# Cross attention: one VectorE instruction takes the score maxima of two heads over two PSUM banks

## The chip, the cores and the metric

The kernel runs on one core of one Trainium2 chip. The metric is the device time of one execution in microseconds (us). The core's engines are TensorE (PE; its weight loads are listed as PEld), VectorE (DVE), ScalarE (ACT), GpSimd (POOL) and SyncE (SP), which issues most DMAs. Each engine works through its own list of instructions in order and waits on semaphores that other engines raise.

## The reference

A decoder layer of 8 batches of 256 tokens and 128 features: self attention with a relative position bias, a cross attention block over 1601 context tokens with 16 heads of size 8, which is followed by a second self attention and a feed-forward part, and at last a mixture of eight experts. The change lies mainly in the first attention of the block:

```python
def _mha(x, ctx, mask, qw, qb, kw, kb, vw, vb):
    q = _split_heads(x @ qw + qb)          # 8 x 256 x 16 heads x 8
    k = _split_heads(ctx @ kw + kb)        # 8 x 1601 x 16 x 8
    v = _split_heads(ctx @ vw + vb)
    scores = jnp.einsum('bqhd,bkhd->bhqk', q, k) / np.sqrt(D // H)
    if mask is not None:
        scores = scores + mask
    probs = jax.nn.softmax(scores, axis=-1)
    out = jnp.einsum('bhqk,bkhd->bqhd', probs, v)
    return out.reshape(x.shape[0], x.shape[1], D)
```

## The kernel before

The kernel runs phase after phase: self attention "A" (with bias), cross attention (`phase_cross`), self attention "S", a tail and the experts. Queries and keys are held as three bf16 parts each, whose products are added by the rows of one matmul; two heads stand in partitions 0 to 53 and 64 to 117 (`half` 0 and 1), so that matmuls of the two halves can run side by side.

Cross attention works through 64 units g (8 batches, `b`, of 8 pairs of heads, `p`). A unit computes its scores twice:

- as **grains**, with the queries on the partitions: 16 products of 128 queries with about 401 keys (2 heads `s`, 2 query tiles `qt`, 4 chunks of the 1601 keys). Each fills one of four PSUM banks (`GRAIN`). VectorE takes the maximum of each (`maxima`, L1436) into `MG`, then `negate` (L1443) joins the chunks' maxima into the negated row maximum, GpSimd's `split_maxima` makes three bf16 parts `MP` of it, TensorE turns these (`max_rows`, "m") and ScalarE copies them into three rows of the queries (`place_maxima`). The maximum is so subtracted by the score product itself.
- as **score tiles**, with the keys on the partitions: 13 tiles of 128 keys (the last has 65). One bank of the ring `RING` (banks 4, 5 and `PX`) takes two products of 256 queries (L1238); ScalarE takes the exponential (`exponentials`, L1356) into `PT`, one of 8 buffers.

The **V products** (L1258) follow in three bursts per unit: tiles 0 to 3, 4 to 7 and 8 to 12, here burst 0, 1 and 2. They add into `k.PO`; ScalarE then copies the sums (`read_sums`, L1372).

The order of all engines' work is one list, `cross_plan(p)`, gone through once per step; each engine takes from it the entries that are its own. An entry ("g", i, 2) in step n belongs to unit n + 2, ("s", t, 0) to unit n, ("m", 0, 1) to unit n + 1. At place j (0 to 12) the list has the score tile j + 3 of the unit (from j = 10 on, tiles 0 to 2 of the next), then a round of preparing the next batch at j = 5 and 10, then, at j = 3, 7 and 12, a burst, with "m" ahead of burst 1, and then one or two grains. So two grains stand right behind burst 0 and two behind burst 1. The rounds by step of a batch: turning the context in steps 0 and 1, keys in 2 and 3, values in 4 and 5, none in 6 and 7. Step 0 also has "c" at j = 1: TensorE's batch sums (L228), VectorE's reciprocal and product (L1449, L1451). The ring's banks go in turn to scores, "m", "c" and rounds, so each of these waits until what had the bank three turns before has been read.

`grain(g, u)` waits until the maximum of the grain four before has been taken. `grain_order` writes out which head and chunk each grain has, so that halves alternate on TensorE.

In self attention "A" a unit has four grains with VectorE's maxima in `MG` (L988); VectorE negates them into `MN` (`negate`, L1001) and GpSimd splits them (L1028 to L1045). "S" negates in the reduction itself (L994).

Of the kernel before, what the change touches and what calls it, by code (L numbers as in the profile page):

```python
# [115 lines left out]
def allocate(k):  # L116
# [20 lines left out]
    k.BANK = [k.stack.enter_context(nc.psum_tensor(f"bank{i}", [128, 512], F32)) for i in range(8)]  # L137
    k.RING = [bank[:, :] for bank in k.BANK]
# [612 lines left out]
def phase_self(k, name):  # L751
# [12 lines left out]
    dve_plan = [("g", 0, 3), ("g", 1, 3), ("g", 2, 3), ("m", 0, 2), ("g", 3, 3), ("neg", 0, 3), ("c", 0, 0)]  # L764
# [20 lines left out]
    with ExitStack() as st:  # L785
# [181 lines left out]
        def _(v):  # L967
# [47 lines left out]
            if bias:  # L1015
                actions["neg"] = negate
            else:
                actions["m"] = lambda u, i: copy_maxima(nc.vector.tensor_copy, v, u, (1,), m_rows_second)
# [3 lines left out]
        def _(pl):  # L1022
# [7 lines left out]
            def split_maxima(u, i):  # L1030
                if bias:
                    pl.wait_ge(neg_ready, u + 1)
                else:
# [25 lines left out]
def cross_plan(p):  # L1059
# [3 lines left out]
    T, G, LEAD = NTILES, 16, 3  # L1063
# [4 lines left out]
    for j in range(T):  # L1068
# [6 lines left out]
        if j == 1 and p == 0:  # L1075
            plan.append(("c", 0, 0))
        if j in bursts:
            if bursts[j] == 1:
                plan.append(("m", 0, 1))
            plan.append(("v", bursts[j], 0))  # L1080
        plan += [("g", g, 2) for g in range(G * (j + 1) // T if j else 0, min(G, G * (j + 2) // T))]
    return plan + [("o", 0, 0), ("neg", 0, 2), ("split", 0, 2)]


def grain_order(chunks):

    rest = [[(s, qt, u, a, w) for qt in range(QT) for u, (a, w) in enumerate(chunks)] for s in range(2)]
# [34 lines left out]
def phase_cross(k):  # L1122

    nc = k.nc
    T, N, G = NTILES, NCTX, 16
# [9 lines left out]
    NG = len(GRAIN)  # L1135
# [9 lines left out]
    with ExitStack() as st:  # L1145
# [6 lines left out]
        MG = k.sb("MG", [128, 4, 4, 4], stack=st)  # L1152
# [32 lines left out]
        def _(pe):  # L1185
# [20 lines left out]
            def grain(g, u):  # L1206
                n = G * g + u
                b, p = batch_of(g)
                s, qt, _, a, w = grains[u]
                half = slice(HALF * s, HALF * s + CROSS_ROWS)  # L1210
                if n >= NG:
                    pe.wait_ge(m_read, n - NG + 1)
# [3 lines left out]
                if p == 0 and u == 0 and b % 2 == 0:  # L1216
                    pe.wait_ge(qk_in[b // 2], Q_LOADS)
                if u == 0:
# [208 lines left out]
        def _(v):  # L1427
            nc.vector.memset(k.PO[:, :], 0.0).then_inc(psum_cleared, 1)

            def maxima(g, u):  # L1430
                n = G * g + u
                s, qt, chunk, a, w = grains[u]
                if u == 0 and g >= 4:
                    v.wait_ge(neg_ready, g - 3)
                v.wait_ge(m_ready, n + 1)
                nc.vector.tensor_reduce(MG[:, g % 4, 2 * s + qt, chunk:chunk + 1], GRAIN[n % NG][:, 0:w],  # L1436
                                        AX.X, ALU.max).then_inc(m_read, 1)

            def negate(g, i):
# [3 lines left out]
                nc.vector.tensor_reduce(MN[:, g % 4, :], MG[:, g % 4, :, :], AX.X, ALU.max,  # L1443
# [912 lines left out]
```

## Time and profile before

| | before |
|---|---|
| median of 3 runs | 1321.23 us (1316.71 to 1325.92) |
| span of the profiled execution | 1324.9 us |
| mean TensorE clock granted | 0.924 of full speed |
| PE busy | 1104.3 us (83%) |
| DVE busy | 1018.2 us (77%) |
| ACT busy | 869.6 us (66%) |
| POOL busy | 403.8 us (30%) |

The time of the profiled execution itself is not listed apart from its span; the span lies inside the range of the three runs. Busy time of an engine counts each moment once, though instructions overlap at their ends; a single instruction's duration runs from its start to its end. Start times are counted from the start of the span. The words in brackets at the end of a timeline row are the engine's idle time ahead of it and what ended it.

### The profile page before, as it was taken

Reading aid. Unit: us, or ns where it says so; the run is one execution under the profiler, and the core shown is the slowest. Engines: PE = TensorE matmul, PEld = TensorE weight load, DVE = VectorE, ACT = ScalarE, POOL = GpSimd, SP = SyncE. Lnnn points to the kernel's source line nnn. Section 1 sums busy time; section 2 is a strip of 40 time slices with the busy share of each in tenths; the row PEclk is TensorE's granted clock in tenths of the full one; section 3 lists DMA queues with packets and bytes.
Section 4 is the critical chain, followed back from the end, with each engine's and each line's share of the span. In section 5 each row is a group of like instructions: output and inputs, shape, how many; then the busy total and the mean of one; then the engine's idle time right before and its main releaser. Section 6 shows DMA issues by size and latency. Waiting matters only on the chain. (4 is left out here: it accounts for less than half of the span.)

```text
span 1324.9 us, 33276 instructions
## 1 busy us (share of the span) xinstructions
PE 1104.3 (83%) x12028; PEld 602.7 (45%) x12028; DVE 1018.2 (77%) x2779; ACT 869.6 (66%) x1764; POOL 403.8 (30%) x832
## 2 busy tenths in 40 slices
PE   5799995699999999999999999986688878178894
PEld 2344443244444444444444444433344436167773
DVE  7488857588889898898988889956699968755554
ACT  3488873187887878788788787882488744233443
POOL 3211113223050320405023040021624227545552
PEclk9699997699999999999999999997799989588997
DMA  6970005513232132311323113002740022111113
GB/s 164 213 144 30 2 2 138 133 56 84 67 82 68 39 93 84 72 57 34 101 78 81 49 30 85 21 2 58 149 87 2 2 96 72 56 29 39 39 37 111
DMA packets 76648, 92.31 MB, mean 70 GB/s; under 512 B 8463, under 2 KB 62711, under 8 KB 76488
## 3 DMA queue, kind: packets, MB, share of 16 engines
q1 hardware_dynamic: 72392, 83.90, 25.1%
q0 software_dynamic: 2496, 5.12, 1.5%
q8 instruction: 98, 1.61, 0.5%
q10 hardware_dynamic: 1600, 1.18, 0.3%
q14 instruction: 62, 0.51, 0.1%
HBM read 64.37 MB, written 27.02 MB: 69 GB/s over the span
## 5 line engine op out<-in xcount | busy, mean ns | idle before, releaser
L1436 DVE TENSOR_REDUCE MG<-bank 128x1 f32<-128x401 f32 (+1 forms) x1024 | 515.4, 566 | 75.3 <-PE bank L1220 73.6
L1356 ACT ACTIVATE PT<-bank 128x512 f32<-128x512 f32 (+1 forms) x624 | 334.6, 597 | 64.3 <-PE bank L1238 63.8
L1238 PE MATMUL bank<-QP,KP 54*128 54x256 bf16 (+1 forms) x1664 | 252.4, 274 | 16.3 <-DVE CAT L1451 4.1
L1220 PE MATMUL bank<-KP,QP 54*128 54x401 bf16 (+1 forms) x1024 | 237.0, 344 | 14.8 <-DMA KP<-ctx_k_parts 9.6
L1258 PE MATMUL bank<-PT,VP 128*9 128x256 f32 (+1 forms) x2688 | 197.3, 367 | 0.8 <-ACT XT L1356 0.8
L1511 POOL TENSOR_TENSOR MP<-MN,ZERO 128x4 bf16<-128x4 f32 x128 | 26.4, 206 | 440.8 <-DVE MN L1443 435.8
L1238 PEld LDWEIGHTS bank<-QP,KP 54*128 54x128 bf16 (+1 forms) x1664 | 110.4, 96 | 108.3 <-ACT PT L1356 24.4
L1220 PEld LDWEIGHTS bank<-KP,QP 54*128 54x128 bf16 x1024 | 75.5, 94 | 125.0 <-DVE MG L1436 94.4
L1356 ACT ACTIVATE XT<-bank 128x512 f32<-128x512 f32 (+1 forms) x208 | 116.2, 599 | 20.3 <-PE bank L1238 19.9
L896 PE MATMUL bank<-QP,KP 51*128 51x256 bf16 x512 | 95.7, 281 | 33.6 <-ACT QP L827 8.8
L1258 PEld LDWEIGHTS bank<-PT,VP 128*9 128x9 f32 (+1 forms) x2688 | 76.0, 90 | 57.6 <-issue 20.4
L863 PE MATMUL bank<-KP,QP 51*128 51x256 bf16 x512 | 97.8, 287 | 4.3 <-DVE MN L994 1.4
L988 DVE CUSTOM_DVE_ANT_0 JUNK<-bank,UQ 128x256 bf16<-128x256 f32 x256 | 92.1, 420 | 6.8 <-PE bank L863 6.6
L951 ACT ACTIVATE XT<-bank 128x512 f32<-128x512 f32 x128 | 74.1, 604 | 32.6 <-PE bank L896 32.0
L1258 PE MATMUL bank<-XT,VP 128*9 128x256 f32 (+1 forms) x896 | 91.2, 367 | 0.0
L994 DVE TENSOR_REDUCE MN<-bank 128x2 f32<-128x512 f32 x128 | 81.8, 685 | 4.2 <-POOL MP L1045 1.2
L1028 POOL TENSOR_TENSOR MP<-MN,ZERO 128x8 bf16<-128x8 f32 x128 | 26.4, 206 | 187.8 <-DVE MN L1001 112.4
L896 PEld LDWEIGHTS bank<-QP,KP 51*128 51x128 bf16 x512 | 33.2, 95 | 103.4 <-issue 43.4
L2041 PE MATMUL bank<-WUP,XP 128*128 x234 | 67.8, 427 | 14.6 <-DVE XP L2210 13.5
L827 ACT COPY QP<-bank 3x512 bf16<-3x512 bf16 x96 | 54.8, 571 | 32.4 <-PE bank L932 32.0
L1364 ACT COPY QP<-bank 3x256 bf16<-3x256 bf16 x128 | 45.3, 354 | 26.5 <-DMA q_parts<-PT 25.7
L2218 DVE TENSOR_TENSOR AC<-SI,bank 128x512 f32<-128x512 f32 x39 | 26.8, 688 | 45.5 <-issue 20.7
(281 smaller groups left out, 2007.5 us busy)
## 6 DMA issues: line engine op xcount, KB each, us to landing
KP<-ctx_k_parts SPq DMA_DIRECT2D x128, 100.1 KB
ctx_k_parts<-KPARTS SPq DMA_DIRECT2D x16, 600.4 KB
KP<-ctx_k_parts SPq DMA_DIRECT2D x128, 59.4 KB
CN<-in_ctx SPq DMA_DIRECT2D x8, 768.0 KB
RAW<-in_w_gate_up SPq DMA_DIRECT2D x8, 512.0 KB, 3.8
QP<-q_parts SPq DMA_DIRECT2D x20, 192.0 KB
ctx_k_parts<-KPARTS SPq DMA_DIRECT2D x16, 200.1 KB
UQ<-bias_table SPq DMA_DIRECT2D x4, 768.0 KB, 8.5
```

The source lines that it names most:

```text
L827: last = copy(k.QP[rows, p:p + 2, b * S:(b + 1) * S], PM[:, :].bitcast(BF16)[rows, 0:2 * S].rearrange("r (j n) -> r j n", j=2))
L863: last = nc.tensor.matmul(bank[:, S * qt:S * (qt + 1)], k.QP[rows, p, a:a + 128], k.KP[rows, p, b * S:(b + 1) * S], start=True, stop=True)
L896: last = nc.tensor.matmul(bank[:, S * t:S * (t + 1)], k.KP[half(s), p, a:a + 128], k.QP[half(s), p, b * S:(b + 1) * S], start=not bias, st ...
L951: nc.scalar.activation(PT[n % 8], SCORE[n % 3][:, :], ACT.Exp).then_inc(exp_done, 1)
L988: last = nc.vector.tensor_tensor_reduce(out=JUNK[:, 2 * (n % 2) + q, :], in0=bank[:, S * q:S * (q + 1)], in1=k.UQ[:, 2 * p + s, 128 * q:12 ...
L994: nc.vector.tensor_reduce(MN[:, u % 3, j, s, :], bank[:, :].rearrange("p (q n) -> p q n", q=QT), AX.X, ALU.max, negate=True).then_inc(grai ...
L1220: nc.tensor.matmul(GRAIN[n % NG][:, 0:w], k.QP[half, p, b * S + 128 * qt:b * S + 128 * (qt + 1)], k.KP[half, p, a:a + w], start=True, stop ...
L1238: return nc.tensor.matmul(bank[0:rows[t], S * at:S * (at + 1)], k.KP[half, p, 128 * t:128 * t + rows[t]], k.QP[half, p, b * S:(b + 1) * S] ...
L1258: last = nc.tensor.matmul(k.PO[32 * c:32 * c + HD + 1, q:q + w], VP[b % 2][0:rows[t], t, 2 * p + s, :], PT[(T * g + n) % NP][0:rows[t], S ...
L1356: nc.scalar.activation(PT[n % NP][0:rows[t], :], bank_of("s", g, t)[0:rows[t], :], ACT.Exp).then_inc(exp_done, 1)
L1436: nc.vector.tensor_reduce(MG[:, g % 4, 2 * s + qt, chunk:chunk + 1], GRAIN[n % NG][:, 0:w], AX.X, ALU.max).then_inc(m_read, 1)
L2041: last = nc.tensor.matmul(bank[j % 2], XP[:, j % 2, a, :], WUP[:, bass.ds(e, 1), b, n0:n0 + FF].rearrange("p a n -> p (a n)"), start=(n == ...
```

## The change

1. Banks 0 to 3 are allocated as one tensor `k.FOUR`, so that an instruction can read two neighbouring banks. `DOUBLE` are its two halves.
2. In cross attention a grain is now a double: the products of both heads for one query tile and one chunk, one in each bank of `DOUBLE[n % 2]`. A unit has 8 instead of 16. TensorE waits once, until the double two before has been read, and signals once, with the second product. VectorE takes both maxima with one reduction of 128x2x401. `MG` is laid out anew for it.
3. `cross_plan` names the places of the doubles: after the scores of j = 0, 1, 3, 4, 6, 7, 9 and 11 and ahead of what else stands there, so that doubles 2 and 5 stand ahead of bursts 0 and 1, and nothing of the kind stands behind a burst. "neg" and "split", which closed a step with unit n + 2, now come after the first double of the next step.
4. In self attention "A" the negation is done by GpSimd, at the head of `split_maxima`, instead of VectorE.

```diff
-    k.BANK = [k.stack.enter_context(nc.psum_tensor(f"bank{i}", [128, 512], F32)) for i in range(8)]
+    k.FOUR = k.stack.enter_context(nc.psum_tensor("bank", [128, 4, 512], F32))
+    more = [k.stack.enter_context(nc.psum_tensor(f"bank{i}", [128, 512], F32)) for i in range(4, 8)]
+    k.BANK = [k.FOUR[:, i, :] for i in range(4)] + [bank[:, :] for bank in more]
...
-    dve_plan = [("g", 0, 3), ("g", 1, 3), ("g", 2, 3), ("m", 0, 2), ("g", 3, 3), ("neg", 0, 3), ("c", 0, 0)]
+    dve_plan = [("g", 0, 3), ("g", 1, 3), ("g", 2, 3), ("m", 0, 2), ("g", 3, 3), ("c", 0, 0)]
...
-            def negate(u, i):
-                v.wait_ge(grain_read, 4 * u + 4)
-                if u >= 3:
-                    v.wait_ge(max_split, 4 * (u - 2))
-                nc.vector.tensor_scalar(MN[:, u % 3, :, :, :], MG[:, u % 3, :, :, :], -1.0, None,
-                                        ALU.mult).then_inc(neg_ready, 1)
...
             def split_maxima(u, i):
-                if bias:
-                    pl.wait_ge(neg_ready, u + 1)
-                else:
-                    pl.wait_ge(grain_read, 4 * u + 4)
+                pl.wait_ge(grain_read, 4 * u + 4)
                 if u >= 3:
                     pl.wait_ge(m_turned, u - 2)
+                if bias:
+                    flat = MG[:, u % 3, :, :, :].rearrange("p j s q -> p (j s q)")
+                    nc.gpsimd.tensor_tensor(MN[:, u % 3, :, :, :].rearrange("p j s q -> p (j s q)"),
+                                            ZERO[:, :].broadcast_to(list(flat.shape)), flat,
+                                            ALU.subtract).then_inc(neg_ready, 1)
+                    pl.wait_ge(neg_ready, u + 1)
...
-    T, G, LEAD = NTILES, 16, 3
+    T, LEAD = NTILES, 3
+    doubles = {0: 0, 1: 1, 3: 2, 4: 3, 6: 4, 7: 5, 9: 6, 11: 7}
...
+        if j in doubles:
+            plan.append(("g", doubles[j], 2))
+        if j == 0:
+            plan += [("neg", 0, 1), ("split", 0, 1)]
         if j in bursts:
             if bursts[j] == 1:
                 plan.append(("m", 0, 1))
             plan.append(("v", bursts[j], 0))
-        plan += [("g", g, 2) for g in range(G * (j + 1) // T if j else 0, min(G, G * (j + 2) // T))]
-    return plan + [("o", 0, 0), ("neg", 0, 2), ("split", 0, 2)]
+    return plan + [("o", 0, 0)]
...
     order, half = [], 0
-    for what, i, _ in cross_plan(PAIRS - 1):
+    for what, d, _ in cross_plan(PAIRS - 1):
         if what == "s":
-            half = 1 - i % 2 if i < NTILES - 1 else 0
+            half = 1 - d % 2 if d < NTILES - 1 else 0
         if what == "g":
-            order.append((rest[half] or rest[1 - half]).pop(0))
-            half = 1 - half
+            order.append((half, *places[d]))
...
-                if n >= NG:
-                    pe.wait_ge(m_read, n - NG + 1)
+                if n >= 2:
+                    pe.wait_ge(m_read, n - 1)
...
-                nc.tensor.matmul(GRAIN[n % NG][:, 0:w], k.QP[half, p, b * S + 128 * qt:b * S + 128 * (qt + 1)],
-                                 k.KP[half, p, a:a + w], start=True, stop=True).then_inc(m_ready, 1)
+                for s in (first, 1 - first):
+                    half = slice(HALF * s, HALF * s + CROSS_ROWS)
+                    last = nc.tensor.matmul(DOUBLE[n % 2][:, s, 0:w],
+                                            k.QP[half, p, b * S + 128 * qt:b * S + 128 * (qt + 1)],
+                                            k.KP[half, p, a:a + w], start=True, stop=True)
+                last.then_inc(m_ready, 1)
...
-                nc.vector.tensor_reduce(MG[:, g % 4, 2 * s + qt, chunk:chunk + 1], GRAIN[n % NG][:, 0:w],
+                nc.vector.tensor_reduce(MG[:, g % 4, :, qt, chunk], DOUBLE[n % 2][:, :, 0:w],
                                         AX.X, ALU.max).then_inc(m_read, 1)
```

## Rows read from the trace of the kernel before

**Rows 1.** Windows: busy us of each engine, granted clock, DMA share, GB/s.
```profile
265.00:925.00 660.00, 607.38 (x7121) 293.05 (x7119) 562.38 (x1238) 518.93 (x1087) 159.56 (x373) 0.98 0.23 62
```

**Rows 2.** Waits from 300 to 900 us: who for whom, total, times, longest.
```profile
PEld bank L1220 <- DVE MG L1436: 79.5, 192, 0.6
...
DVE MG L1436 <- PE bank L1220: 57.7, 135, 1.5
```

**Rows 3.** Timeline of PE in a plain step: start, us, instructions.
```profile
407.53 0.62 PE L1258 MATMUL bank<-XT,VP 128*9 128x256 f32 x8
...
408.52 0.34 PE L1220 MATMUL bank<-KP,QP 54*128 54x401 bf16 x2
...
408.70 0.27 PE L1238 MATMUL bank<-QP,KP 54*128 54x256 bf16 x1
...
409.77 0.39 PE L1238 MATMUL bank<-QP,KP 54*128 54x256 bf16 x2
...
410.36 0.40 PE L1258 MATMUL bank<-PT,VP 128*9 128x256 f32 x2
...
412.91 0.82 PE L1220 MATMUL bank<-KP,QP 54*128 54x401 bf16 x2
...
413.72 0.62 PE L1258 MATMUL bank<-XT,VP 128*9 128x256 f32 x8
...
414.92 0.28 PE L1238 MATMUL bank<-QP,KP 54*128 54x256 bf16 x1
```

**Rows 4.** Timeline of ACT in the same step.
```profile
409.11 0.60 ACT L1356 ACTIVATE PT<-bank 128x512 f32<-128x512 f32 x1 [0.48 <-PE bank L1238]
...
412.02 2.52 ACT L1356 ACTIVATE PT<-bank 128x512 f32<-128x512 f32 x5 [0.26 <-PE bank L1238]
415.06 0.37 ACT L1372 COPY OT<-bank 128x256 f32<-128x256 f32 x1 [0.52 <-PE bank L1258]
```

**Rows 5.** Timeline of DVE in the same step.
```profile
406.47 0.17 DVE L1443 TENSOR_REDUCE MN<-MG 128x4 f32<-128x16 f32 x1
...
408.90 2.50 DVE L1436 TENSOR_REDUCE MG<-bank 128x1 f32<-128x401 f32 x5 [0.21 <-PE bank L1220]
411.80 3.46 DVE L1436 TENSOR_REDUCE MG<-bank 128x1 f32<-128x401 f32 x7 [0.40 <-PE bank L1220]
```

**Rows 6.** The page's groups of instructions: busy us, mean ns, idle before.
```profile
L1436 DVE TENSOR_REDUCE MG<-bank 128x1 f32<-128x401 f32 (+1 forms) x1024 | 515.4, 566 | 75.3 <-PE bank L1220 73.6
...
L994 DVE TENSOR_REDUCE MN<-bank 128x2 f32<-128x512 f32 x128 | 81.8, 685 | 4.2 <-POOL MP L1045 1.2
```

**Rows 7.** Timeline of ACT: the copies of the sums, one a step.
```profile
343.82 0.37 ACT L1372 COPY OT<-bank 128x256 f32<-128x256 f32 x1 [0.51 <-PE bank L1258]
...
356.00 0.37 ACT L1372 COPY OT<-bank 128x256 f32<-128x256 f32 x1 [0.40 <-PE bank L1258]
...
365.49 0.37 ACT L1372 COPY OT<-bank 128x256 f32<-128x256 f32 x1 [0.63 <-PE bank L1258]
...
385.47 0.37 ACT L1372 COPY OT<-bank 128x256 f32<-128x256 f32 x1 [0.49 <-PE bank L1258]
...
396.19 0.37 ACT L1372 COPY OT<-bank 128x256 f32<-128x256 f32 x1 [0.49 <-PE bank L1258]
...
406.27 0.37 ACT L1372 COPY OT<-bank 128x256 f32<-128x256 f32 x1 [0.58 <-PE bank L1258]
```

**Rows 8.** Timeline of PE in a batch's first step and in a values step.
```profile
348.53 0.39 PE L1238 MATMUL bank<-QP,KP 54*128 54x256 bf16 x2 [0.58 <-DVE CAT L1451]
...
390.61 0.23 PE L1269 MATMUL bank<-IDB,MP 128*3 128x128 bf16 x2 [0.57 <-DVE VP L1461]
```

**Rows 9.** Timeline of DVE in a batch's first step.
```profile
348.38 2.01 DVE L1436 TENSOR_REDUCE MG<-bank 128x1 f32<-128x401 f32 x4
```

**Rows 10.** Timeline of POOL: last operation of a split.
```profile
407.57 0.21 POOL L1524 TENSOR_TENSOR MP<-MN,MP 128x4 bf16<-128x4 f32 x1
```

**Rows 11.** Timeline of DVE in self attention "A", behind the negation.
```profile
147.39 0.06 DVE L986 MEMSET TOUCH<- 1x1 f32 x1 [0.90 <-PE bank L863]
```

More of the change, by code:

```diff
@@ L136, in allocate @@
     k.HALF = k.sb("HALF", [128, NT])
-    k.BANK = [k.stack.enter_context(nc.psum_tensor(f"bank{i}", [128, 512], F32)) for i in range(8)]
-    k.RING = [bank[:, :] for bank in k.BANK]
+    k.FOUR = k.stack.enter_context(nc.psum_tensor("bank", [128, 4, 512], F32))
+    more = [k.stack.enter_context(nc.psum_tensor(f"bank{i}", [128, 512], F32)) for i in range(4, 8)]
+    k.BANK = [k.FOUR[:, i, :] for i in range(4)] + [bank[:, :] for bank in more]
+    k.RING = list(k.BANK)
     k.PO, k.PX = k.BANK[6], k.BANK[7]
@@ L1014, in _ @@
             actions = {"g": maxima, "c": divide}
-            if bias:
-                actions["neg"] = negate
-            else:
+            if not bias:
                 actions["m"] = lambda u, i: copy_maxima(nc.vector.tensor_copy, v, u, (1,), m_rows_second)
@@ L1080, in cross_plan @@
             plan.append(("v", bursts[j], 0))
-        plan += [("g", g, 2) for g in range(G * (j + 1) // T if j else 0, min(G, G * (j + 2) // T))]
-    return plan + [("o", 0, 0), ("neg", 0, 2), ("split", 0, 2)]
+    return plan + [("o", 0, 0)]
 def grain_order(chunks):
-    rest = [[(s, qt, u, a, w) for qt in range(QT) for u, (a, w) in enumerate(chunks)] for s in range(2)]
+    places = [(qt, u, a, w) for qt in range(QT) for u, (a, w) in enumerate(chunks)]
     order, half = [], 0
-    for what, i, _ in cross_plan(PAIRS - 1):
+    for what, d, _ in cross_plan(PAIRS - 1):
         if what == "s":
-            half = 1 - i % 2 if i < NTILES - 1 else 0
+            half = 1 - d % 2 if d < NTILES - 1 else 0
         if what == "g":
-            order.append((rest[half] or rest[1 - half]).pop(0))
-            half = 1 - half
+            order.append((half, *places[d]))
     return order
@@ L1124, in phase_cross @@
     nc = k.nc
-    T, N, G = NTILES, NCTX, 16
+    T, N, G = NTILES, NCTX, 8
     rows = [min(128, N - 128 * t) for t in range(T)]
@@ L1204, in take_bank, with grain @@
                 return RING[n % 3]
-            def grain(g, u):
-                n = G * g + u
+            def grain(g, d):
+                n = G * g + d
                 b, p = batch_of(g)
-                s, qt, _, a, w = grains[u]
-                half = slice(HALF * s, HALF * s + CROSS_ROWS)
-                if n >= NG:
-                    pe.wait_ge(m_read, n - NG + 1)
+                first, qt, _, a, w = grains[d]
+                if n >= 2:
+                    pe.wait_ge(m_read, n - 1)
                 if n == 0:
@@ L1215, in grain @@
                     pe.wait_ge(q_taken, 4)
-                if p == 0 and u == 0 and b % 2 == 0:
+                if p == 0 and d == 0 and b % 2 == 0:
                     pe.wait_ge(qk_in[b // 2], Q_LOADS)
-                if u == 0:
+                if d == 0:
                     pe.wait_ge(kp_in[p], LOADS * (b + 1))
-                nc.tensor.matmul(GRAIN[n % NG][:, 0:w], k.QP[half, p, b * S + 128 * qt:b * S + 128 * (qt + 1)],
-                                 k.KP[half, p, a:a + w], start=True, stop=True).then_inc(m_ready, 1)
+                for s in (first, 1 - first):
[4 more added lines that the diff above has]
+                last.then_inc(m_ready, 1)
             def scores(g, i):
@@ L1428, in _, with maxima @@
             nc.vector.memset(k.PO[:, :], 0.0).then_inc(psum_cleared, 1)
[L1430 to L1433, printed above, removed]
+            def maxima(g, d):
+                n = G * g + d
+                _, qt, chunk, a, w = grains[d]
+                if d == 0 and g >= 4:
                     v.wait_ge(neg_ready, g - 3)
                 v.wait_ge(m_ready, n + 1)
-                nc.vector.tensor_reduce(MG[:, g % 4, 2 * s + qt, chunk:chunk + 1], GRAIN[n % NG][:, 0:w],
+                nc.vector.tensor_reduce(MG[:, g % 4, :, qt, chunk], DOUBLE[n % 2][:, :, 0:w],
                                         AX.X, ALU.max).then_inc(m_read, 1)
@@ L1514, in split_maxima @@
                 pl.wait_ge(neg_ready, g + 1)
+                x, parts = MN[:, g % 4, :], [MP[:, g % 4, :, a] for a in range(3)]
                 if g >= 4:
                     pl.wait_ge(m_turned, g - 3)
-                x, parts = MN[:, g % 4, :], [MP[:, g % 4, :, a] for a in range(3)]
                 copy(parts[0], x).then_inc(max_split, 1)
```

10 lines of the change are left out of this document (4 added, 6 removed).

## The prediction

> **What bounds the kernel now.** I read the trace from coarse to fine: the windows, the waits, then one step of each kind in the timelines. Only cross attention matters for most of the change, and it is the stretch from 265 to 925 us. VectorE is busy there for 562 of 660 us, TensorE for 607, ScalarE for 519 [rows 1]. None is full, so the order of waits decides. The waits go round in a circle: TensorE's weight loads for grains wait 79.5 us for maxima, and the maxima wait 57.7 us for grains [rows 2]. A saving on either engine is worth something only where its wait ends last.
>
> So I took one plain step (no round of the next batch) and measured from the start of burst 2, at 404.93, which is 8.79 before the row at 413.72 [rows 3]. Below, times after a + sign count from the last start of burst 2, and Vn is burst n. V0 starts at 407.53, +2.60. It stands behind the score of tile 6, which waits for the exponential of tile 3, which waits for the copy of the sums at V2 +1.34 (415.06 against 413.72) [rows 3, 4]. V1 starts at 410.36, +5.43, through score 7, its exponential at 409.11 and the next exponential, for which the bank of the transposed maxima waits [rows 3, 4]. V2 starts at 413.72, +8.79. It is held by grain 15 (the second of the two at 412.91, which start 0.48 apart), which is started only when the maximum of grain 11 is out; the chain of exponentials alone (412.02, the next 0.48 later) would have let tile 2's score, and with it V2, start 0.26 sooner [rows 3 to 5]. VectorE has gaps of its own in this step: before a run of five reads and before a run of seven it waits 0.21 and 0.40 us beyond the tail of a read [rows 5]. Both lie behind bursts. The loop is thus mostly TensorE to ScalarE and back; VectorE closes it only before V2.
>
> **The reads.** Seven reads take 3.46 us, five 2.50 [rows 5]: (3.46 - 2.50)/2 = 0.48 us from start to start, against 0.566 from start to end [rows 6]. A read of 512 columns takes 0.685 [rows 6], so a column costs (685 - 566)/111 = 1.07 ns. A double adds 401 columns: 0.99 us to its end, 0.91 to the next start. Eight save 8 x (0.966 - 0.91) = 0.45 us of VectorE a step. No row has a read over two banks. One bound is the time of two reads, 0.48 + 0.566 = 1.05, or 1.13 if both pay in full; the other is 0.89, if 0.03 of the 0.119 us between the two forms is the price of L994's second output and a column costs 0.80 ns. I take 0.99, as L994 is nearest: it too reads two runs and writes two maxima.
>
> The Trainium skill, "Perfetto Trace Analysis", Optimizing Scalar/DVE Operations, gives VectorE about 125 ns of overhead per instruction on PSUM and advises grouping where the engine is saturated; it also says that where an engine is not saturated but makes others wait, smaller instructions let work finish sooner, which speaks against this change. Starts 0.48 us apart for 401 columns leave 0.05 to 0.07 us of overhead that blocks the next read, half of what the page gives; by the page 8 x 0.125 = 1.0 us of VectorE a step would be saved, an estimate from that page.
>
> **What is later: V0.** In the new order D0 follows score 3, D1 score 4, and D2 stands after score 6, ahead of V0. D2 uses D0's banks and waits for D0's read. TensorE returns from V2 at +1.20 (414.92 against 413.72) [rows 3]. D0's second half waits for two score products of 0.11 each, starts at +1.42, takes 0.34 and is seen 0.04 later: VectorE reads D0 from +1.80 to +2.79. D2 starts 0.06 later (TensorE's delay after such a wait: an exponential ends at 409.11 + 0.60, the score that waits for it starts at 409.77 [rows 3, 4]) and V0 0.26 behind it (its 0.17 of streaming and 0.09 of change-over). V0: +3.11 instead of +2.60, 0.50 later. In exchange the pair of grains between V0 and score 7 is gone, which costs 408.70 - 408.52 = 0.18 [rows 3]: score 7 is 0.32 later.
>
> **V1.** In a plain step score 7's exponential and the next would allow V1 0.32 later. But D5, which now stands before the maxima's transposes and V1, waits for the read of D3. D3 starts after V0: ready at V0 + 0.98 + 0.22 + 0.38 = +4.69, read by +5.68, D5 at +5.74, V1 0.28 later: +6.02, so 0.57 to 0.59 later. The pair behind V1 (0.18) is gone too: scores 11 and 12 are 0.39 later.
>
> **V2.** The 0.26 of slack in the exponentials takes part of the 0.39, since D7 waits for D5's read, long out. Plain step: +0.14. That is 19 steps (two in each of seven batches, five in the last, not counting two steps that make no maxima).
>
> **Steps with rounds** have these periods, between copies of the sums [rows 7]: 12.18, 9.49, twice 9.99, 10.72, 10.08. In them V1 waits for the round's own chain (its bank must be taken before the maxima's transposes: idle 0.57 behind VP [rows 8]), which starts 0.18 sooner behind V0 as the pair is gone, so V1 is 0.50 - 0.18 = 0.32 later and score 11 is 0.14 later. Where the last part is set by the exponentials (the second and sixth step) the step is +0.14. Where it is set by TensorE after the second round (third to fifth), three single grains become one double: 0.34 is won there, -0.20 each. In the first step VectorE's reciprocal and product hold the bank of score 7 until 348.53, 0.15 after the next read starts [rows 8, 9]. D3 now stands between scores 7 and 8 and waits for D1's whole read, 0.99 from 348.38: score 8 starts 0.41 later, V1 0.57, score 11 0.39; 0.13 of slack remains, +0.26. The last batch has this step without rounds: +0.6, since nothing hides D5's wait.
>
> **Sum.** A batch: 0.26 + 0.14 - 0.20 x 3 + 0.14 + 0.14 x 2 = +0.22; seven give +1.6, the last 0.6 + 5 x 0.14 = +1.3. Cross attention: +2.9 us.
>
> **Edits that cost nothing.** "neg" and its split follow D0 now, one read later. The split ends 1.31 us after the negation starts (407.57 + 0.21 against 406.47 [rows 5, 10]), so at about +4.0, and its reader stands ahead of V1 near +6. The order of halves stays alternating, and the two halves of a double run side by side as two grains did (two in 0.34 us [rows 3]). In the first attention VectorE's negation goes, 32 of 0.17 us, and GpSimd does one more operation of 0.2 us for a unit. VectorE waits 0.90 us for grains right after that negation [rows 11], so the 0.17 ends as longer idle time; the split is late by 0.08 to 0.1 and is read 1.5 us after it is done. Without that cover 32 x 0.1 = 3 us either way. The key loads follow scores, and the POOL and SP queues keep their order.
>
> The profiled span is 1324.9 us; the runs have 1316.7 to 1325.9 and no time stands with that execution itself. A difference carries over: 1321.2 + 2.9 = 1324.
>
> **Rivals.** (a) Faster: VectorE is the bound, as the 79.5 us of weight loads behind maxima suggest [rows 2]. Then a step gains 0.45 us, x 62 = 28: 1293. Against it stand VectorE's own 57.7 us of waits and its gaps behind V0 and V1. By the skill's overhead, 1.0 us a step, it would be about 60 us, an estimate from "Perfetto Trace Analysis"; the row at 3.46 us for seven reads disagrees.
> (b) Faster: D2 and D5 find their banks free, because D0 is read sooner than I walk, and only the two pairs behind the bursts are gone. 2 x 0.18 x 62 = 22 us: 1299. Against it: D0 cannot start before V2 is through, and its read alone takes about one microsecond.
> (c) Slower: a read over two banks costs as much as two, 1.13 us. The place is D0's read before V0, once in each of 62 steps, and D3's (or D1's) read again in the 27 plain and first steps: 89 x 0.14 = 12 us on top of 2.9: 1336. It decides from about 1.1 us a read. For it: nothing in the trace shows such a read. Against it: L994 reads in two runs with no extra price per run.
> (d) The change does not do what it says if the doubles are read as two instructions; that is the price of (c) at 1.05, 1329, and lies in the range.
>
> **Chances.** Forecast with (d) 0.61, its own range 1314 to 1332; (a) 0.08; (b) 0.11; (c) 0.20. A measurement of this kernel tells about 1% from no change, its three runs being 0.7% apart, so the forecast counts as same, (a) and (b) as faster and (c) as slower. The range 1298 to 1338 takes in (b), the forecast and (c), and leaves (a) out.
>
> **What would show it.** In the profile after: 512 reads at L1436's place of 0.99 us; V0 3.1 us behind the start of V2 in steps without batch sums; V1 6.0 behind V2 in plain steps and 0.3 later than before in steps with rounds; periods of 8.9 in plain steps and 9.8 in the steps that make keys; VectorE with less busy time (by about 30 us) and more waiting for TensorE; L1001's negation gone with the first attention as long as before. The forecast is wrong if V0 stays at 2.6, or if the read is not near 0.99.

## The result, and the profile after

After the change the kernel takes 1334.0 us (median of 4 runs, 1331.2 to 1336.9), before it 1320.9 (4 runs beside them, 1316.7 to 1325.9): a ratio of 1.010, 95% interval 1.0066 to 1.0132, so about 13 us slower. The forecast was 2.9 us slower. The profiled executions span 1329.4 and 1324.9 us, only 4.5 apart, because the one of after came to cross attention 3.7 us earlier (first V product at 262.4 instead of 266.1) and was 3.7 us shorter behind it. Neither is put down to the change: over all twelve traces, whose kernels hardly differ outside cross attention, the first V product comes between 261.9 and 266.1, and what stands behind the last burst takes 423.7 to 429.9 us. Between the first start of burst 0 and the last start of burst 2 it took 640.7 us instead of 628.9. These 11.8 us are to be explained.

The page of after, its parts 1 and 5. VectorE is busy 977.4 us, 40.8 less than before, and the reads over two banks take 988 ns:

```profile
PE 1089.8 (82%) x12028; PEld 592.9 (45%) x12028; DVE 977.4 (74%) x2235; ACT 870.2 (65%) x1764; POOL 412.8 (31%) x864
...
L1438 DVE TENSOR_REDUCE MG<-bank 128x2 f32<-128x802 f32 (+1 forms) x512 | 489.6, 988 | 120.3 <-PE bank L1220 117.6
```

The windows (busy us of each engine, granted clock, DMA share, GB/s) over cross attention, where VectorE was busy 85% of the time [rows 1] and is now busy 79%:

```profile
265.00:903.00 638.00, 582.74 (x6976) 275.77 (x6975) 504.94 (x660) 510.39 (x1069) 154.13 (x364) 0.99 0.22 61
```

The waits from 300 to 900 us:

```profile
DVE MG L1438 <- PE bank L1220: 99.7, 153, 2.0
...
PEld bank L1220 <- DVE MG L1438: 45.3, 85, 0.8
...
PE bank L1220 <- DVE MG L1438: 20.8, 79, 0.6
```

TensorE waits less for maxima, 45.3 + 20.8 us where the weight loads alone had 79.5, while VectorE waits 99.7 us for scores instead of 57.7 [rows 2]. VectorE has become cheaper and waits more, yet the whole is longer. The totals can't say why, as they don't tell which of the waits a burst stands behind. That is seen only in a step.

TensorE in a plain step. Burst 2 starts at 410.25, D0 at 411.46 and 411.68, D2 at 413.17, V0 at 413.45, D5 at 416.07, V1 at 416.36, V2 at 419.30:

```profile
410.25 0.62 PE L1260 MATMUL bank<-XT,VP 128*9 128x256 f32 x8
...
411.45 0.28 PE L1240 MATMUL bank<-QP,KP 54*128 54x256 bf16 x1
...
411.68 0.33 PE L1220 MATMUL bank<-KP,QP 54*128 54x401 bf16 x1
...
413.17 0.34 PE L1220 MATMUL bank<-KP,QP 54*128 54x401 bf16 x2 [0.25 <-DVE MG L1438]
413.45 0.81 PE L1260 MATMUL bank<-PT,VP 128*9 128x256 f32 x9
...
416.07 0.34 PE L1220 MATMUL bank<-KP,QP 54*128 54x401 bf16 x2 [0.17 <-DVE MG L1438]
...
416.36 0.40 PE L1260 MATMUL bank<-PT,VP 128*9 128x256 f32 x2
...
419.30 0.62 PE L1260 MATMUL bank<-PT,VP 128*9 128x256 f32 x8
```

VectorE in the same step:

```profile
412.12 0.99 DVE L1438 TENSOR_REDUCE MG<-bank 128x2 f32<-128x802 f32 x1 [0.87 <-PE bank L1220]
413.03 0.16 DVE L1445 TENSOR_REDUCE MN<-MG 128x4 f32<-128x16 f32 x1
413.11 4.71 DVE L1438 TENSOR_REDUCE MG<-bank 128x2 f32<-128x802 f32 x5
418.40 1.89 DVE L1438 TENSOR_REDUCE MG<-bank 128x2 f32<-128x802 f32 x2 [0.59 <-PE bank L1220]
```

VectorE stands idle for 0.87 us until D0 is computed, reads it until 413.11, and 0.06 us after that D2 starts, with V0 0.28 behind it. (The group of 4.71 us from 413.11 is five reads, of which the first is D1's.) The "[0.25 <-DVE MG L1438]" in the row of D2 and the "[0.17 ...]" in that of D5 are the two new places at which all of TensorE stands still for VectorE. Relative to V2:

| plain step | before | forecast | after |
|---|---|---|---|
| D0's read starts | - | +1.80 | +1.87 |
| V0 | +2.60 | +3.11 | +3.20 |
| V1 | +5.43 | +6.02 | +6.11 |
| V2 (the period) | +8.78 | +8.92 | +9.05 |

The copies of the sums by ScalarE, one a step, to set against those of before [rows 7]:

```profile
339.36 0.37 ACT L1374 COPY OT<-bank 128x256 f32<-128x256 f32 x1 [0.26 <-PE bank L1260]
...
351.80 0.37 ACT L1374 COPY OT<-bank 128x256 f32<-128x256 f32 x1 [0.26 <-PE bank L1260]
...
361.54 0.37 ACT L1374 COPY OT<-bank 128x256 f32<-128x256 f32 x1 [0.63 <-PE bank L1260]
...
371.45 0.37 ACT L1374 COPY OT<-bank 128x256 f32<-128x256 f32 x1 [0.16 <-PE bank L1260]
...
392.00 0.37 ACT L1374 COPY OT<-bank 128x256 f32<-128x256 f32 x1 [0.32 <-PE bank L1260]
...
402.34 0.37 ACT L1374 COPY OT<-bank 128x256 f32<-128x256 f32 x1 [0.63 <-PE bank L1260]
...
411.59 0.37 ACT L1374 COPY OT<-bank 128x256 f32<-128x256 f32 x1 [0.27 <-PE bank L1260]
```

The copies don't all wait alike, so I take the periods below from the starts of burst 2 in the trace's timeline of TensorE. They repeat from batch to batch to 0.02 us wherever the clock is full and no transfer is awaited:

| step of a batch | 0 | 1 | 2 | 3 | 4 | 5 | 6 | 7 | batch |
|---|---|---|---|---|---|---|---|---|---|
| before | 12.17 | 9.49 | 9.99 | 9.99 | 10.72 | 10.08 | 8.78 | 8.78 | 80.0 |
| after | 12.44 | 9.75 | 9.91 | 9.91 | 10.64 | 10.34 | 9.05 | 9.05 | 81.1 |
| difference | +0.27 | +0.26 | -0.08 | -0.08 | -0.08 | +0.26 | +0.27 | +0.27 | +1.1 |
| forecast | +0.26 | +0.14 | -0.20 | -0.20 | -0.20 | +0.14 | +0.14 | +0.14 | +0.2 |

The batches from the second to the last took 1.27, 1.07, 2.37, 2.83, 1.06, 0.99 and 3.03 us longer than the same ones of before. 1.07 is the table's step pattern. Most of what lies above it is in first steps of 13.75 to 13.77 us instead of 12.44, in the fourth, fifth and seventh batch (the seventh has such a step before the change too, 13.58 for 12.17, so the difference there is only 0.99), and in that of the last; two seventh steps add 0.2 and 0.4. The windows of two first steps after, each from V0 to just ahead of V2, at full clock and at reduced clock, and the last part of the latter, from V1 on; the column behind the busy times is the granted clock:

```profile
423.60:431.70 8.10, 6.62 (x74) 3.12 (x72) 7.22 (x9) 6.24 (x13) 0.00 (x0) 1.00 0.15 48
504.70:514.10 9.40, 7.95 (x74) 3.52 (x72) 7.17 (x9) 6.26 (x13) 0.00 (x0) 0.82 0.23 70
509.54:514.14 4.60, 4.51 (x40) 2.07 (x39) 2.41 (x4) 3.09 (x9) 0.00 (x0) 0.66 0.28 86
```

These two windows hold the same 74 matmuls and the same 9 and 13 operations of VectorE and ScalarE, and the second is 1.3 us longer. TensorE is busy 1.33 us more in it, the other two no more than in the first. TensorE ran part of it at the lower of its two levels, 1.2 GHz instead of 2.4. Before the change the same happened once in seven first steps (the windows of before):

```profile
426.60:434.70 8.10, 7.10 (x80) 3.35 (x81) 7.53 (x14) 6.53 (x14) 0.00 (x0) 1.00 0.16 49
746.70:756.10 9.40, 8.46 (x76) 3.74 (x74) 7.61 (x14) 6.69 (x14) 0.00 (x0) 0.82 0.13 45
```

After it, four times in seven, the last one in the eighth batch (13.07 us, granted clock 0.87). What a first step has ahead of that part is in the timelines of VectorE and TensorE, here of the one at full clock; the one with the fall has the same two stops of TensorE, 0.69 and 0.51 us:

```profile
423.06 1.76 DVE L1451 RECIPROCAL REC<-bank 128x256 f32<-128x256 f32 x1 [0.82 <-PE bank L230]
```

```profile
425.34 0.39 PE L1240 MATMUL bank<-QP,KP 54*128 54x256 bf16 x2 [0.70 <-DVE CAT L1453]
...
426.24 0.34 PE L1220 MATMUL bank<-KP,QP 54*128 54x398 bf16 x2 [0.51 <-DVE MG L1438]
```

The reciprocal runs ahead of D1's read, and with it VectorE's product (0.42 us), which frees the bank of score 7. TensorE stands still for 0.70 us for the bank of score 7, and right after it for another 0.51 us, which is new, for D1's read. Before, the first wait is there with 0.58 us [rows 8].

### The profile page after: what moved, and what is told of

It is laid out like the page before. It is cut to its first block and busy times, and to the rows that moved or that the text cites. A ratio compares the mean times of both kernels' runs of the same rounds, so it can differ in the third digit from the quotient of the medians.

```text
span 1329.4 us, 32735 instructions
## 1 busy us (share of the span) xinstructions
PE 1089.8 (82%) x12028; PEld 592.9 (45%) x12028; DVE 977.4 (74%) x2235; ACT 870.2 (65%) x1764; POOL 412.8 (31%) x864
## 5 line engine op out<-in xcount | busy, mean ns | idle before, releaser
L1438 DVE TENSOR_REDUCE MG<-bank 128x2 f32<-128x802 f32 (+1 forms) x512 | 489.6, 988 | 120.3 <-PE bank L1220 117.6
L1240 PE MATMUL bank<-QP,KP 54*128 54x256 bf16 (+1 forms) x1664 | 265.7, 276 | 25.8 <-DVE CAT L1453 4.9
L1220 PE MATMUL bank<-KP,QP 54*128 54x401 bf16 (+1 forms) x1024 | 221.2, 344 | 36.5 <-DVE MG L1438 26.5
L1240 PEld LDWEIGHTS bank<-QP,KP 54*128 54x128 bf16 (+1 forms) x1664 | 99.7, 95 | 188.9 <-ACT PT L1358 90.4
L1513 POOL TENSOR_TENSOR MP<-MN,ZERO 128x4 bf16<-128x4 f32 x128 | 26.4, 206 | 461.0 <-DVE MN L1445 456.0
L2102 ACT ACTIVATE SI<-bank 128x512 f32<-128x512 f32 x39 | 23.3, 598 | 54.5 <-PE bank L2043 45.2
```

Source lines behind the costliest of these rows:

```text
L1220: last = nc.tensor.matmul(DOUBLE[n % 2][:, s, 0:w], k.QP[half, p, b * S + 128 * qt:b * S + 128 * (qt + 1)], k.KP[half, p, a:a + w], start= ...
L1240: return nc.tensor.matmul(bank[0:rows[t], S * at:S * (at + 1)], k.KP[half, p, 128 * t:128 * t + rows[t]], k.QP[half, p, b * S:(b + 1) * S] ...
L1438: nc.vector.tensor_reduce(MG[:, g % 4, :, qt, chunk], DOUBLE[n % 2][:, :, 0:w], AX.X, ALU.max).then_inc(m_read, 1)
```

## The experiments

The theory that I took into them, from here on W: **the cost is the wait of D2 for the read of D0, which holds V0, and that of D5 for the read of D3, which holds V1**. Rivals: O, the order is the whole cost and the width of the read nothing; R, the width of the read matters, since each waiting product waits for both banks; N, the negation on GpSimd costs something.

### 1. The negation alone

The kernel before, with the change's fourth part only: in self attention "A" GpSimd negates.

```diff
-dve_plan = [("g", 0, 3), ("g", 1, 3), ("g", 2, 3), ("m", 0, 2), ("g", 3, 3), ("neg", 0, 3), ("c", 0, 0)]
+dve_plan = [("g", 0, 3), ("g", 1, 3), ("g", 2, 3), ("m", 0, 2), ("g", 3, 3), ("c", 0, 0)]
...
+                    nc.gpsimd.tensor_tensor(MN[:, u % 3, :, :, :].rearrange("p j s q -> p (j s q)"),
+                                            ZERO[:, :].broadcast_to(list(flat.shape)), flat,
+                                            ALU.subtract).then_inc(neg_ready, 1)
```

> The kernel before with part 4 of the change alone: GpSimd negates the maxima of self attention A. Theory W (the doubles ahead of bursts 0 and 1 wait for reads of VectorE and hold the bursts): this part costs nothing, 1321 within 3 us, self attention A as long as before. Rival A (the negation on GpSimd costs part of the 13 us): 1325 or more.

Measured: 1321.2 us (10 runs), ratio 0.999 (0.997 to 1.0011), and every step of cross attention as before. The window of self attention "A" in this kernel, and then in the one before:

```profile
40.00:187.00 147.00, 133.35 (x1916) 63.63 (x1916) 106.81 (x647) 113.80 (x211) 32.88 (x160) 0.92 0.36 79
```

```profile
40.00:187.00 147.00, 133.33 (x1912) 63.88 (x1916) 112.70 (x685) 113.72 (x210) 26.98 (x130) 0.92 0.37 79
```

VectorE has 5.9 us less to do in it, GpSimd 5.9 more, and TensorE, which is 91% busy, does the same work in the same time. The negation costs nothing, so N falls, and the whole cost lies in cross attention.

### 2. Each double read by two reductions

```diff
-                nc.vector.tensor_reduce(MG[:, g % 4, :, qt, chunk], DOUBLE[n % 2][:, :, 0:w],
-                                        AX.X, ALU.max).then_inc(m_read, 1)
+                for s in (0, 1):
+                    last = nc.vector.tensor_reduce(MG[:, g % 4, s:s + 1, qt, chunk], DOUBLE[n % 2][:, s, 0:w],
+                                                   AX.X, ALU.max)
+                last.then_inc(m_read, 1)
```

> The changed kernel, but each double is read by two instructions of one bank each, and only the second signals. Theory W: the pair takes 0.48 + 0.57 = 1.05 us instead of 0.99, so burst 0 starts 0.06 later (3.26 us behind the start of burst 2) and in plain steps burst 1 another 0.06: plain step 9.17, in all 1334 + 6 = 1340. Rival L (an instruction over two banks is itself what costs): faster than the changed kernel, near 1325.

Measured: 1335.0 us, 1.0116 (1.0073 to 1.0159). A plain step takes 9.17 us, V0 at +3.26. The new wait in the timeline of TensorE:

```profile
491.24 0.34 PE L1220 MATMUL bank<-KP,QP 54*128 54x401 bf16 x2 [0.31 <-DVE MG L1439]
```

D2 waits 0.31 us instead of 0.25, as the two reads end 0.06 us later than the one. A batch at full clock takes 81.8 us, 0.75 more than after the change. The steps came as expected. The total, expected at 1340, came out 5 us lower: in the profiled execution this kernel had two falls of the clock in first steps against four, and the interval is some 6 us to either side. As a price of the wide read, 0.988 us against 1.05, it is worth 0.06 us in each of the two waits, and only because those waits are there.

### 3. The order alone

The kernel before, with its single reads and four single banks, and the grains at the places of the change.

```diff
+    doubles = {0: 0, 1: 1, 3: 2, 4: 3, 6: 4, 7: 5, 9: 6, 11: 7}
...
+        if j in doubles:
+            plan += [("g", 2 * doubles[j], 2), ("g", 2 * doubles[j] + 1, 2)]
+        if j == 0:
+            plan += [("neg", 0, 1), ("split", 0, 1)]
...
-        plan += [("g", g, 2) for g in range(G * (j + 1) // T if j else 0, min(G, G * (j + 2) // T))]
-    return plan + [("o", 0, 0), ("neg", 0, 2), ("split", 0, 2)]
+    return plan + [("o", 0, 0)]
```

> The kernel before with single grains, four banks and one read a grain, but the places of the change: two grains where a double stands, ahead of the bursts, and the negation after the first two. Theory W: the second grain ahead of burst 0 waits only for the second read, which ends 0.17 sooner than a double's: burst 0 at 3.03 behind burst 2 instead of 3.20, burst 1 at 2.82 behind it instead of 2.92, plain step 8.8, in all about 1324. Rival O (the order alone is the whole cost, the double nothing): 1334, plain step 9.05.

Measured: 1334.8 us, 1.0111 (1.007 to 1.0151). A plain step takes 9.03 us, V0 at +3.12. TensorE around the wait, V2 being at 484.21, and VectorE's reads for it:

```profile
487.05 0.34 PE L1224 MATMUL bank<-KP,QP 54*128 54x401 bf16 x1
...
487.32 0.62 PE L1262 MATMUL bank<-XT,VP 128*9 128x256 f32 x8
...
490.30 0.40 PE L1262 MATMUL bank<-PT,VP 128*9 128x256 f32 x2
```

```profile
485.94 1.06 DVE L1440 TENSOR_REDUCE MG<-bank 128x1 f32<-128x401 f32 x2 [1.02 <-PE bank L1224]
```

Two single reads, begun with the first half of D0, end at 487.00, +2.79. The second grain of the pair ahead of V0 starts 0.05 later. I had expected 8.8 us from W, with this pair costing less than the double, and O's 9.0 came. So **the order is the whole cost**: with half-wide reads and four banks to itself the order costs as much as the change (a batch at full clock takes 80.9 us against 81.1). R falls. The wait that W names is still there; it is only nearly as long for the second of two single reads (V0 at +3.12) as for one wide one (+3.20).

### 4. Both waiting doubles behind their bursts

```diff
-    doubles = {0: 0, 1: 1, 3: 2, 4: 3, 6: 4, 7: 5, 9: 6, 11: 7}
+    doubles = {0: 0, 1: 1, 4: 3, 6: 4, 9: 6, 11: 7}
+    behind = {3: 2, 7: 5}
...
+        if j in behind:
+            plan.append(("g", behind[j], 2))
```

> The changed kernel with doubles 2 and 5 directly behind bursts 0 and 1 instead of ahead of them. Theory W: burst 0 is back at 2.60 behind burst 2, burst 1 at about 2.97 behind it (score 10 now waits behind double 4), burst 2 at 3.11: plain step 8.68, in all 1316 to 1320. Rival L (the read over two banks is the cost): still above 1330.

Measured: 1323.4 us, 0.9995 (0.9967 to 1.0024), as fast as before. A plain step takes 8.63 us, V0 at +2.60 and V1 at +5.53: both waits are gone, the step is 0.42 shorter than after the change and 0.15 shorter than before. The total is above the 1316 to 1320 expected. A first step took 12.46 us at full clock, but five of seven had a fall of the clock and took 13.03 to 13.78. In first steps V0 to V1 is still 4.75 us (before 4.32), as D3 waits for D1's read behind the reciprocal. The sixth step of a batch also takes 10.40 instead of 10.08, so that even at full clock a batch is 79.9 us, hardly less than the 80.0 of before.

### 5 and 6. One of the two behind its burst

Number 5 has D2 behind V0 and D5 ahead of V1, number 6 the reverse.

```diff
+    doubles = {0: 0, 1: 1, 4: 3, 6: 4, 7: 5, 9: 6, 11: 7}
+    behind = {3: 2}
```

```diff
+    doubles = {0: 0, 1: 1, 3: 2, 4: 3, 6: 4, 9: 6, 11: 7}
+    behind = {7: 5}
```

> The changed kernel with double 2 alone moved behind burst 0; double 5 stays ahead of burst 1. Theory W with one read per wait: burst 0 is back at 2.60 behind burst 2, but double 3 now comes later for VectorE, so the wait of double 5 grows: burst 1 at 3.65 behind burst 0 (before 2.83, changed 2.92), burst 2 at 2.93: plain step 9.18, 0.13 more than the changed kernel; in all 1333 to 1338. Rival H (whatever stands ahead of burst 0 costs its own price, independent of double 5): plain step 8.45, in all below 1315.

> The changed kernel with double 5 alone moved behind burst 1; double 2 stays ahead of burst 0. Theory W: burst 0 stays at 3.20 behind burst 2, burst 1 at 2.65 (the exponentials), burst 2 at 3.10 (the pair costs 0.18 there again): plain step 8.95, in all 1329 to 1333. Rival H: double 5 is the whole cost and the plain step is 8.6 or less.

Measured: number 5 takes 1331.7 us, 1.007 (1.0048 to 1.0093), number 6 takes 1335.9, 1.0115 (1.008 to 1.015). In the plain step, with V0, V1 and the period: number 5 has 2.60, 6.21, 9.14; number 6 has 3.20, 5.86, 8.96. In number 5 V0 is back at its place and V1 is even later than after the change. Its rows of D4, D5 and V1, V2 being at 485.10:

```profile
490.12 0.34 PE L1223 MATMUL bank<-KP,QP 54*128 54x401 bf16 x2 [0.49 <-DVE MG L1441]
491.02 0.34 PE L1223 MATMUL bank<-KP,QP 54*128 54x401 bf16 x2 [0.33 <-DVE MG L1441]
491.31 0.40 PE L1263 MATMUL bank<-PT,VP 128*9 128x256 f32 x2
```

D2's products now come 1.0 us behind the start of V0, at +3.59 instead of +2.92, so its read and that of D3 behind it end later: D4 waits 0.49 us for the read of D2, and D5 0.33 for that of D3. The two waits are each real and don't add up: each alone costs about what both cost (8.96 and 9.14 against 9.05), both away give 8.63. In number 6 V0's 0.60 is there in full, by D2's wait. The plain steps came within 0.04 us of what W expected. The total of number 5 is a little under its expectation of 1333 to 1338; V1 comes 0.1 to 0.2 us sooner in its steps with rounds than after the change, and these steps are as much shorter. The total of number 6 is above its expectation of 1329 to 1333, because the steps with rounds got 0.17 longer: there V1 waits for the round's chain, not for D5, so the doubles moved behind V1 cost their 0.17 us of TensorE and buy nothing.

### 7. The batch sums behind D1

The change, with "c" behind D1 in the first step, so that D1's read comes ahead of the reciprocal.

```diff
-        if j == 1 and p == 0:
-            plan.append(("c", 0, 0))
         if j in doubles:
             plan.append(("g", doubles[j], 2))
+        if j == 1 and p == 0:
+            plan.append(("c", 0, 0))
```

> The changed kernel with the batch sums and VectorE's reciprocal behind double 1 instead of ahead of it, so that double 3 no longer waits for a read that stands behind the reciprocal. Theory W: in a batch's first step score 8 starts some 0.7 sooner, the step is 11.8 to 12.0 instead of 12.44, other steps unchanged. Theory C (the granted TensorE clock falls in first steps because TensorE stands idle there longer than before, 1.3 us each time, 4 of 7 times in the changed kernel and 1 of 7 before): at most one first step shows it now, in all 1334 - 4 - 4 = 1326. Rival: the falls come as often as in the changed kernel, in all 1330.

Measured: 1327.4 us (10 runs), 1.0048 (1.0027 to 1.0068), some 6 us less than after the change. The first step takes 11.72 us instead of 12.44, a little less than the 11.8 to 12.0 expected, all other steps are the same, and all seven first steps show a granted clock of 1.00. TensorE in a first step, and the window of it:

```profile
426.60 0.28 PE L1240 MATMUL bank<-QP,KP 54*128 54x256 bf16 x1 [0.86 <-DVE CAT L1453]
426.61 0.34 PE L1220 MATMUL bank<-KP,QP 54*128 54x398 bf16 x1
```

```profile
424.70:432.20 7.50, 6.51 (x78) 3.18 (x80) 6.57 (x8) 6.08 (x14) 0.00 (x0) 1.00 0.16 49
```

The bank of score 7 comes as late as ever, but D3 starts with it instead of 0.9 us behind it, as D1 has been read. This saves 0.72 us in each of six first steps; the eighth batch's goes from 13.07 to 11.17, of which 0.8 at full clock. The duration from the first V0 to the last V2 is 630.3 us, 10.4 less than after the change: 6 x 0.72 + 0.8 = 5.1 from these periods, 3 x 1.3 + 1.1 = 5.0 from falls of the clock that are gone, and 0.6 in two seventh steps, less 0.3 in the very first unit. The trace is of an execution that took 1321.4 us, the shortest of the ten (up to 1333.1); whether the others had falls, no trace shows.

### 8. The same in the kernel before

```diff
-        if j == 1 and p == 0:
-            plan.append(("c", 0, 0))
...
         plan += [("g", g, 2) for g in range(G * (j + 1) // T if j else 0, min(G, G * (j + 2) // T))]
+        if j == 1 and p == 0:
+            plan.append(("c", 0, 0))
```

> The kernel before with one edit: batch sums and reciprocal behind the grain of place 1 instead of ahead of it. The grain that score 8 stands behind then waits for a read ahead of the reciprocal's. Theory W: first step 11.6 to 11.9 instead of 12.17, in all 1318 to 1320. Rival: the first step stays at 12.17, as its length is the reciprocal's chain.

Measured: 1318.8 us (10 runs), 0.9967 (0.9944 to 0.999). The first step takes 12.02 us instead of 12.17, less of a gain than expected, and none of the seven shows a fall. This place of "c" was worth 0.15 us in the kernel before and 0.72 after the change: it was the change that put a wait for D1's read close behind the reciprocal.

### 9. An order without the waits

The change's wide reads, with every double at a place where its banks were read long before: D3 after j = 5, D4 ahead of V1, D2 and D5 behind their bursts, "c" behind D1.

```diff
-    doubles = {0: 0, 1: 1, 3: 2, 4: 3, 6: 4, 7: 5, 9: 6, 11: 7}
+    doubles = {0: 0, 1: 1, 5: 3, 7: 4, 9: 6, 11: 7}
+    behind = {3: 2, 7: 5}
```

> Doubles where their waits are covered: 0 and 1 as in the change, 2 directly behind burst 0, 3 behind the round of place 5, 4 behind score 10, 5 directly behind burst 1, 6 and 7 as they were, and the batch sums behind double 1. Theory W: first step 11.75, then 9.5, 9.66, 9.66, 10.39, 10.08, 8.53, 8.53: 78.1 a batch against 80.0 before and 81.1 in the changed kernel; in all about 1308, 1.1% under the kernel before. Rival L (the double itself, its longer read and single signal, costs something wherever it stands): not faster than before, 1321 or more.

Measured: **1302.1 us** (6 runs), 0.9855 (0.9819 to 0.989), 20 us faster than before and 32 faster than the change. Periods: 11.89, 9.50, 9.58, 9.58, 10.21, 9.91, 8.53, 8.53, sum 77.7; plain step V0 at +2.60, V1 at +5.43, both as before, and V2 0.25 sooner, which is the slack of 0.26 that grain 15 had held. The total is 6 us under the expected 1308, the batch 0.4 under the expected 78.1. No first step shows a fall, and from 300 to 880 us the profile has no product of TensorE that waits for a maximum. What it meets next is in the timeline of TensorE in a seventh step:

```profile
556.19 0.35 PE L1223 MATMUL bank<-KP,QP 54*128 54x401 bf16 x2 [1.05 <-DMA KP<-ctx_k_parts]
```

The grains of the next batch wait for its keys. The seventh steps of four batches are 0.07 to 0.9 us longer than 8.53.

### 10. This order with single reads

The order of number 9 in the kernel of number 3: single reads, single banks.

> The places of the tuned order (e9), but single grains in four banks, two wherever a double stands. It says what of the tuned kernel's 20 us is the order's and what the double's. Theory W: VectorE has 0.5 us more to do in a step, of which about half shows, since the tuned order leaves it few gaps: plain step 8.55 to 8.8, in all 1302 to 1312. Rival D (the double makes the gain): back at the kernel before, 1320.

Measured: 1308.3 us (6 runs), 0.9886 (0.9854 to 0.9918); the intervals of 9 and 10 overlap. The periods are the same to 0.01 us in all eight steps, 77.8 a batch. What differs is in seventh steps (9.31, 8.90, 10.09, 8.98 and 8.91 us in the second to sixth batch against 9.12, 8.55, 9.44, 9.05 and 8.53), where TensorE waits for keys. With the order put right the read over two banks is worth nothing in any step, although it takes 33 us of VectorE's busy time away (1009.4 against 976.9, of which 6.0 are the negation of self attention "A", as experiment 1 shows). The medians differ by 6 us, more than the 1.6 us between the two traces in cross attention; with six runs each and these intervals that is not told apart from noise, nor is a gain of some us ruled out.

## Why the prediction was right, and where it was off

The measured 1334.0 is slower by 0.99%, just within the bound of 1% that counted as the same, and within the range of 1298 to 1338; it is 2 us above the forecast's own range of 1314 to 1332. The mechanism was the right one, its size was too small: +2.9 forecast, +11.8 in cross attention. That 1334 lies in the range is in part luck: the range reaches so high for the sake of rival (c), a read as dear as two, which is not what happened, and some 3.7 us of what cross attention lost from its second batch on are the clock, for which the forecast had no term.

- **The reads**: forecast 0.99 us, measured 0.988. VectorE got 40.8 us cheaper (forecast 30), and this did not shorten the loop. 26.4 of it are the wide reads (experiment 2, with two reads in the place of one, is busy 1003.8 us against 977.4), close to the 28 forecast, and 6.0 the negation in "A" (experiment 1). The rest, 8.4, goes with the negation in cross attention, 64 of 0.17 us, which now stands between reads that follow each other and overlaps them; the forecast had no term for it. The Trainium skill, "Perfetto Trace Analysis", Optimizing Scalar/DVE Operations, gives about 125 ns of overhead for a VectorE instruction on PSUM; here 512 reads fewer saved 26.4 us of busy time, 52 ns each. That section of the Trainium skill advises grouping where the engine is saturated; here VectorE was busy 85% of the time, and grouping gave no step anything.
- **V0**: right in its chain (D0's products, D0's read, D2, V0). The term was mis-sized: forecast +0.50, measured +0.60. VectorE started D0's read 0.11 us after the product's modelled end (412.12 against 411.68 + 0.33), where I had taken 0.04. 0.04 is what the read of D6 shows in the same trace, with VectorE idle just as well ahead of it, and in the trace of before the read of grain 0 starts 0.18 behind its product and that of grain 9 0.04. So the delay goes with the place, for a reason that no run shows, and the row of the grain at D0's own place would have been the one to take it from.
- **V1**: right, forecast 0.57 to 0.59 later and 6.02, measured 6.11, the 0.09 of V0 passed on. Experiments 5 and 6 show the two waits one by one.
- **V2**: here the step of the sum failed. "Takes part of the 0.39" left +0.14, measured +0.27 in plain steps; +0.26 instead of +0.14 in the second and sixth, -0.08 instead of -0.20 in the third to fifth. It is the same 0.12 to 0.13 us in 54 steps (19 plain, 35 with rounds), 6.6 us in all. 0.09 of it is V0's. I walked V0 to 0.01 us where no row had such a wait, and the sum is a difference of terms four times as large, so it had the uncertainty of that walk 54 times over; the range of the forecast should have carried it.
- **First step**: forecast +0.26, measured +0.27, with D3 behind D1's read as its cause (experiment 7). The last batch's: forecast +0.6, measured +1.7, of which 1.1 us is the clock. That is an estimate: at full clock V1 comes at +9.03 and V2, as in a plain step, 2.94 behind it, which makes 11.97 and +0.6 (the same sum gives 12.15 for experiment 2, which had no fall there, and 12.15 was measured).
- **The clock** was no term at all: 3 x 1.3 us less the 1.4 that before had too, and about 1.1 in the last batch, 3.7 us net. Two seventh steps add 0.2 and 0.4 us at full clock; in the second of the two D0 waits 0.25 us for a transfer of keys.
- **The account** for the second to the last batch: 6 x 1.07 of the steps' pattern, 1.9 in the last batch at full clock (0.6 + 5 x 0.26), 3.7 of clock and 0.6, together 12.6; measured 12.6, forecast 6 x 0.22 + 1.3 = 2.6. The first batch, from its first V0, was 0.8 us shorter than before: its first unit took 7.03 us from V0 to V2 at a granted clock of 0.93, before 8.55 at 0.78, and its other steps were 0.7 longer; that gives the 11.8.
- **Edits that cost nothing**: right (experiment 1); the place of the negation in cross attention was never seen to be waited for.
- **Rivals**: (a) falls, as VectorE lost 41 us and waited 42 us more. (b) falls, D2 and D5 do wait. (c) and (d) fall, as the read takes 0.988 us and two reads in its place cost 0.75 us a batch.

Open: what makes the clock fall. One execution of each kernel was traced. Five kernels have two long stops of TensorE in their first steps, 0.6 to 0.7 us for the bank of score 7 and 0.5 to 0.6 for D1's read: the change and those of experiments 2, 4, 5 and 6. Of their 35 first steps 16 show a fall (4, 2, 5, 4 and 1). Six kernels have only the first (0.6 to 0.9 us), before and experiments 1 and 7 to 10, and 2 falls in 42. The kernel of experiment 3 has no long second stop either, as its single grains start one by one when the single reads end, and yet 3 falls in 7. A first step of it with a fall:

```profile
671.16 0.39 PE L1242 MATMUL bank<-QP,KP 54*128 54x256 bf16 x2 [0.69 <-DVE CAT L1455]
671.64 0.82 PE L1224 MATMUL bank<-KP,QP 54*128 54x398 bf16 x2
672.13 0.39 PE L1242 MATMUL bank<-QP,KP 54*128 54x256 bf16 x2
```

Behind the stop of 0.69 us only 0.09 and 0.14 are left ahead of 671.64 and 672.13. So the falls go with grains that wait for a read behind the reciprocal, but a second long stop isn't needed for them; why the kernel of number 6 had one and that of number 4 five is not settled, and no run varied the length of a stop by itself.

## What to carry to other kernels

Work put ahead of a burst puts its own wait ahead of the burst too. So for each moved product ask when the read that frees its bank ends, and if that read is still to come at the new place, the burst waits for it whatever engine is "less busy". Here the order, the place of the batch sums included, was worth 32 us and fusing two reads into one nothing that a step shows, because VectorE was 85% busy and still not the bound: its time per instruction counts only where TensorE waits for that one read. And when two such waits stand in one loop, take both away: each alone hides the other, so undoing one shows almost nothing.

## What the hardware showed that I had not expected

- TensorE's granted clock can fall inside a phase in which TensorE is 91% busy: 0.82 on average over 9.4 us of a first step and 0.66 over the last 4.6 of it, which costs 1.3 us, in a step that holds stops of 0.7 and 0.5 us. In the changed kernel the next step has its full-clock period again; in the last batch of experiments 3 and 5 the clock was still at 0.93 and 0.91 of full speed there, and the step 0.6 and 0.8 us longer. Where a fall came with it, a first step that the sum had at +0.3 us took 1.6 more.
- VectorE starts the read of D0 0.11 us after the modelled end of the product and that of D6 0.04 after it, idle before both; what makes the difference is not shown.
- A read over two banks takes 0.988 us for 2 x 401 columns, the next one behind it starts 0.90 us later (two take 1.89), and two single reads take 1.06 (experiment 3). Per bank it is thus hardly cheaper: 52 ns of busy time for each instruction saved.
- The reduction into 128 x 4 took 0.17 us as L1443 before [rows 5] and 0.16 as L1445 after; which part of the change did it is not shown.
